# Attention and mixture-of-experts block on one core: layer norms on GpSimd as four instructions with row scalars, larger near score from PSUM in half precision, differences by multiply and add

## The reference

```python
x = x + _layernorm(_L0_attn_ref(_layernorm(x), ...))
x = x + _layernorm(_L0_ffn_ref(_layernorm(x), ...))

def _layernorm(x, axis=-1, eps=1e-05):
    m = jnp.mean(x, axis=axis, keepdims=True)
    v = jnp.var(x, axis=axis, keepdims=True)
    return (x - m) / jnp.sqrt(v + eps)

# attention: 16 heads of 8 features, causal, with relative positions clipped to 2
rel_k = rel_k_table[idx]; rel_v = rel_v_table[idx]
scores = (scores + jnp.einsum('bhqd,qkd->bhqk', Qh, rel_k)) / scale
attn = jax.nn.softmax(jnp.where(causal, scores, -1e9), axis=-1)
out = jnp.einsum('bhqk,bhkd->bhqd', attn, Vh) + jnp.einsum('bhqk,qkd->bhqd', attn, rel_v)
# feed-forward: a shared expert, and two of eight routed experts by a sigmoid router
```

## Time and profile before

| | us |
|---|---|
| median of 3 runs (lowest to highest) | 1051.91 (1050.83 to 1052.38) |
| the profiled execution: time | 1049.69 |
| the profiled execution: span | 1048.0 |
| PE busy in the span | 910.0 (87%) |
| DVE busy | 837.1 (80%) |
| POOL (GpSimd) busy | 729.3 (70%) |
| ACT busy | 675.1 (64%) |

### The profile page before, as it was taken

The page is one execution under the profiler, slowest core; times in us unless marked ns, Lnnn a source line. Parts: engine busy times, 40 slices in busy tenths (PEclk is TensorE's granted clock), DMA queues, the critical chain, the costliest instruction groups (busy, mean ns, idle before and its releaser), DMA issues.

```text
span 1048.0 us, 23476 instructions
## 1 busy us (share of the span) xinstructions
PE 910.0 (87%) x7655; PEld 521.8 (50%) x7655; DVE 837.1 (80%) x1948; ACT 675.1 (64%) x1303; POOL 729.3 (70%) x940
## 2 busy tenths in 40 slices
PE   2768889999999999899999999987289999999995
PEld 0334444444444444444444444432167777777774
DVE  5677888888888988888888888974478887878874
ACT  2137677677767776776777777665047767676773
POOL 4135586876966867768769668555448889898886
PEclk9869999999999999999999999988589999999998
DMA  2610110110101101101101011020325454555540
GB/s 49 167 45 31 35 44 32 45 43 30 51 32 40 47 33 43 45 32 46 42 32 51 31 42 46 22 67 19 100 91 149 154 160 142 168 155 166 163 137 31
DMA packets 64004, 74.93 MB, mean 72 GB/s; under 512 B 10032, under 2 KB 39600, under 8 KB 63904
## 3 DMA queue, kind: packets, MB, share of 16 engines
q1 hardware_dynamic: 61536, 73.17, 22.1%
q10 hardware_dynamic: 2368, 0.48, 0.3%
HBM read 43.75 MB, written 8.65 MB: 50 GB/s over the span
## 4 chain that ended last, share of the span: by engine, by line
PE 44%; DVE 18%; POOL 12%; ACT 12%; issue 6%; SPq 5%; DMA 1%; POOLq 0%; DVEq 0%; ACTq 0%
PE ps_av L1532 10%; DVE mx L1114 7%; PE ps_av L1731 6%; ACT prob L792 6%; POOL prob L634 5%; PE ps_s L1698 5%; PE ps_e L1472 5%; SPq L454 5%; PE ps_misc L1540 4%; PE ps_s L1495 3%; PE ps_e L1698 3%; POOL hidden_low L735 2%; ACT av_s L857 2%; PE ps_s L1516 2%; DVE hidden_low L1368 2%
## 5 line engine op out<-in xcount | busy, mean ns | idle before, releaser
L1114 DVE TENSOR_REDUCE mx<-ps_s 128x1 f32<-128x512 f32 (+2 forms) x640 | 409.4, 684 | 78.3 <-PE ps_s L1516 75.5
L792 ACT ACTIVATE prob<-ps_e 128x512 f32<-128x512 f32 x640 | 347.4, 601 | 118.8 <-PE ps_e L1472 118.8
L634 POOL TENSOR_SCALAR_AFFINE_SELECT prob<-prob 128x516 f32<-128x516 f32 (+1 forms) x320 | 173.1, 565 | 170.0 <-ACT prob L792 170.0
L1495 PE MATMUL ps_s<-ks,qs 63*128 63x512 f16 (+3 forms) x1024 | 214.7, 311 | 21.0 <-DMA ks<-kl 8.3
L1472 PE MATMUL ps_e<-qs,ks 64*128 64x512 f16 (+3 forms) x1024 | 196.5, 303 | 14.7 <-DMA qs<-mT 7.1
L735 POOL TENSOR_TENSOR hidden_low<-hidden,hidden_high 128x512 fp32r<-128x512 f32 x144 | 191.4, 1357 | 20.3 <-ACT hidden_high L981 19.0
L1532 PE MATMUL ps_av<-prob,vp 128*32 128x512 f32 (+3 forms) x2048 | 182.6, 452 | 23.2 <-POOL prob L634 23.0
L981 ACT CAST hidden_high<-hidden 128x512 fp32r<-128x512 f32 x160 | 98.1, 613 | 34.8 <-DVE hidden L1420 30.7
L1472 PEld LDWEIGHTS ps_e<-qs,ks 64*128 64x128 f16 x1024 | 60.8, 95 | 115.5 <-ACT prob L792 64.0
L1516 PE MATMUL ps_s<-masked_at,below_r 64*128 64x128 bf16 (+3 forms) x640 | 106.4, 211 | 0.0
L1495 PEld LDWEIGHTS ps_s<-ks,qs 63*128 63x128 f16 x1024 | 63.5, 94 | 79.6 <-DVE mx L1114 54.9
(11 more groups left out here) (175 smaller groups left out, 1745.0 us busy)
## 6 DMA issues: line engine op xcount, KB each, us to landing
gate_rows<-gates_dram SPq DMA_DIRECT2D x128, 256.0 KB, 3.6
qs<-qh SPq DMA_DIRECT2D x128, 32.0 KB
qs<-ql SPq DMA_DIRECT2D x128, 32.0 KB
xnT_dram<-oT SPq DMA_DIRECT2D x16, 256.0 KB, 2.0
xeT<-xnT_dram SPq DMA_DIRECT2D x16, 256.0 KB, 2.7
out<-result SPq DMA_DIRECT2D x16, 256.0 KB, 2.3
v_near<-v_back SPq DMA_DIRECT2D x16, 254.0 KB
ks<-kh SPq DMA_DIRECT2D x124, 32.0 KB
```

The lines of the kernel that those rows point to most:

```text
L634: pool.affine_select(out=v, in_=v, compare_op=ALU.is_ge, fill=0.0, base=-2, pattern=cols, channel_multiplier=-1).then_inc(S["p_masked"], 1)
L792: act.activation(prob[g % 2][:, u, b, :], ps_e[bank][:, :], ACT.Exp, scale=SCALE).then_inc(S["e_done"], 1)
L1114: dve.tensor_reduce(out, src, AX.X, ALU.max).then_inc(s_free[bank], 1)
L1495: pe.matmul(scores[:, at:at + P * (qt + 1)], qs[par][rows, 2 * g + off, P * qt:P * qt + P], ks[par][rows, 2 * g + off, 0:P * (qt + 1)], st ...
```

## The change

`normalise` no longer subtracts the mean over the whole tile ahead of the power. After the power, four instructions of 128x128, one for each tile of 128 tokens, subtract the mean and multiply by the reciprocal deviation, both given as one scalar for each partition. In `s_tok_out` the maximum of the two near scores reads the first from the copy in SBUF and the second from PSUM, between the two copies, and `s_best` becomes half precision. The differences are `m16 * -1 + s_tok` in a scalar_tensor_tensor instruction in place of a subtraction of two tensors.

```diff
-CHAIN_DVE, CHAIN_POOL = 33, 14
+CHAIN_DVE, CHAIN_POOL = 33, 20
...
-        s_best = sb("s_best", [P, NT, H])
+        s_best = sb("s_best", [P, NT, H], F16)
...
                 own.mark(pool.tensor_scalar(var[:, :], mv[:, :, 1], 1.0, EPS, ALU.mult, ALU.add))
-                own.mark(pool.tensor_tensor(dst, src, mv[:, :, 0:1].to_broadcast([P, NT, P]), ALU.subtract))
                 own.settle()
                 own.mark(pool.tensor_tensor(rs[:, :], var[:, :], neg_half[:, :], ALU.pow))
                 own.settle()
-                return pool.tensor_tensor(dst, dst, rs[:, :].unsqueeze(2).to_broadcast([P, NT, P]), ALU.mult)
+                for i in range(NT):
+                    last = pool.tensor_scalar(dst[:, i], src[:, i], mv[:, i, 0:1], rs[:, i:i + 1], ALU.subtract, ALU.mult)
+                    if i < NT - 1:
+                        own.mark(last)
+                return last
...
-                for n in range(2):
-                    last = dve.tensor_copy(s_tok[:, n], src[:, n])
-                    if n == 0:
-                        own.mark(last)
-                last.then_inc(S["misc_free"], 1)
+                own.mark(dve.tensor_copy(s_tok[:, 0], src[:, 0]))
+                own.settle()
+                own.mark(dve.tensor_tensor(s_best[:, :, :], s_tok[:, 0], src[:, 1], ALU.max))
+                dve.tensor_copy(s_tok[:, 1], src[:, 1]).then_inc(S["misc_free"], 1)
 
                 dve.wait_ge(S["misc_free"], st.misc("s_tok") + 1)
                 own.settle()
-                own.mark(dve.tensor_tensor(s_best[:, :, :], s_tok[:, 0], s_tok[:, 1], ALU.max))
...
-                    last = dve.tensor_tensor(d01[:, k, :, hs], s_tok[:, k, :, hs], m16[:, :, hs], ALU.subtract)
+                    last = dve.scalar_tensor_tensor(d01[:, k, :, hs], m16[:, :, hs], -1.0, s_tok[:, k, :, hs],
+                                                    ALU.mult, ALU.add)
```

## The result

The changed kernel takes 1095.91 us against 1052.09 us: 4.1% slower (ratio 1.0406, 95% interval 1.0389 to 1.0422). The forecast was 1040 us, within 1033 to 1052. One of the four executions of the changed kernel took 2662.7 us at full granted clock; the comparison leaves it out, and nothing here explains it.

A forecast was written before the change was run, and what follows sets the result against it. PE leads but waits 1.47 us per step for GpSimd's masks, queued behind the norms. Savings of 9.4 (14 x 0.67) + 0.67 + 0.67 + 1.3 = 12.0 us take 1051.9 to 1039.9, forecast 1040, range 1033 to 1052.

The forecast's parts named there:

- The duration x of the new instruction: Time of one 128x128 GpSimd subtract-and-multiply with row scalars in each norm: taken as 0.40 us, bounded by 0.293 and 0.632.
- 1.25 + 4x: Length of one changed norm on GpSimd in us, four new instructions included: 2.85 us forecast against 3.52 before.
- The slower rival: Four GpSimd instructions with scalars cost more than two wide passes in each norm: 1058 us at x = 0.63, chance 0.15.
- second and third norm on one path: Beyond break-even both norms lengthen one path through addition, DVE's statistics and masks, slack 0.13 us: 0.39 us a step.
- The first norm gives room only: At the step's first norm, for the next sequence, PE has no wait on GpSimd, so its saving counts nothing.
- Where a saving lands: Which norm's saving shortens the attention step: the loop through the third norm, by 0.67 us per step.
- the bound of 1.47: PE's two waits for GpSimd's masks per step, 0.84 + 0.63 us: the slack of the loop without any norm.
- shorter relief: Savings of the second and third norm do not add in a step; the smaller counts, 0.67 us.
- The second norm's masks are late because of GpSimd's queue and not of ACT: Masks at 514.77 stand behind the second norm on GpSimd, not behind ACT's exponential; could end up to 1.0 us sooner.
- The DVE edits at nothing: Larger near score and differences on DVE: no gain taken, within 0.2 us per step either way for the score.

The follow-up runs named there:

- the last version: Kernel before with the third norm's two wide GpSimd instructions replaced by four 128x128 Identity activations on ACT: 1042.51 us, ratio 0.9912.

## Why the prediction was wrong

- **The duration x of the new instruction** is the step that failed. I took 0.40 us, between the one-input select (0.293) and the two-input 128x256 product (0.632). It is 0.796, outside both. The bound from above was no bound: I let the number of input tensors set the price, and took the select for any one-input instruction. The select runs at 0.95 ns per element, the arithmetic form with scalars at 3.3. With x = 0.796 the sum "1.25 + 4x" gives 4.43 us; 4.55 was measured. The form was right, the term mis-sized by a factor of two, and with it the sign.
- **The slower rival** was the one that came about: it was to decide at x = 0.57 and had a chance of 0.15, but only for x up to 0.63 and 1058 us. Its own rule (second and third norm on one path, 2 x 1.03 - 0.13 = 1.9 us a step, with the ends 30 us) would have given 1082 at the true x.
- **"The first norm gives room only"** failed as well. It was read from a timeline in which PE does not wait there, which excludes a gain and says nothing of a loss. The room was 0.42 us, less than the 1.03 us that the norm grew by. With the first norm alone changed it cost 12 us, which is the size of what 1082 lacks to 1096.
- **PE's clock** was left out. Some stretches of value matmuls behind a wait of PE run at a lower clock, and three of twelve steps of the changed kernel are 0.7 us longer in its company, where one was in the kernel before. That is some 1.4 us of the 44 (3 x 0.7 less 0.74), so it does not carry the result.
- **Where a saving lands** held in size: 1.0 us a step against the bound of 1.47 and the "shorter relief" rule's 1.12. That it is the third norm's loop alone is not shown; with that norm alone relieved the step fell by 0.57 us, and PE then waited for ACT and for the first norm.
- **The second norm's masks are late because of GpSimd's queue and not of ACT**: right. PE's wait there grew from 0.84 to 1.92 us, by 1.08, as the norm grew by 1.03.
- **The DVE edits at nothing**: right. s_best at 0.22 us, and differences that still stretch to 0.66 us. The hold by GpSimd has a price, 5 us in the kernel before, that I had left out.

## What to carry to other kernels

A GpSimd instruction's price goes by its operation and form, not by how many tensors it reads: before replacing wide two-tensor instructions by fused ones with row scalars, run one of the new form. An engine that shows idle time ahead of a loop's wait can absorb a saving and still pass on most of a loss, so each place needs its slack in both directions. A price that no row shows is not bounded by rows of other operations; if the sign hangs on it, the chance of the other side should be near one half.

## What was not expected of the hardware

GpSimd's tensor_scalar on f32 is slower than its tensor_tensor at equal size: 531 against 401 ns at 128x128 with one operation, and 3.3 against 1.7 ns per element in the form used here. The same norm step on ACT, four 128x128 Identity activations with row scale and bias, took 1.64 us against 3.14.

PE's granted clock fell after waits that are short beside a step, at one place above all: the eight value matmuls on the masks behind the second norm. At full clock they take 1.06 us. In the kernel before they once took 1.78 us, behind a wait of 0.85 us; with the new first norm 1.77 us in one step behind 0.88 us and 1.07 us in the step before behind 0.90; with the new second norm 1.94 us behind 1.87 us. In the changed kernel they took 1.07 us behind 1.92 us (548.00 above), and one step earlier, behind the same wait:

```profile
503.19 1.94 PE L1534 MATMUL ps_av<-prob,vp 128*32 128x512 f32 x8 [1.93 <-POOL prob L637]
```

What decides between these was not settled. In the kernel before, in the changed one, with the new first norm and in the last version, steps with a mean clock below 1.00 are 0.7 to 1.5 us longer than those at 1.00; but the first four of the changed kernel and two of those with the new third norm, at 0.96, are not.
